# A three-block perceiver layer on one Trainium2 core: gathers on 64-column tiles, a first feed-forward product in two parts, weight loads and GpSimd's sums in another order

## The reference

```python
h = layernorm(x)
scores = einsum('bsd,d->bs', h, w_router)
top_scores, top_idx = top_k(scores, 32)            # 32 of the 64 rows of each batch
selected = h[top_idx]
y = gelu(selected @ W1 + b1) @ W2 + b2             # 512 -> 2048 -> 512
out = h; out[top_idx] += sigmoid(top_scores) * y
x = x + out
```

## Time and profile before

| | us |
|---|---|
| median of 3 runs | 1370.66 (1370.24 to 1371.76) |
| profiled execution, its own time | 1372.64 |
| span in the profile | 1370.8 |
| TensorE (PE) busy | 1335.4, 97% |
| VectorE (DVE) busy | 670.8, 49% |
| ScalarE (ACT) busy | 728.8, 53% |
| GpSimd (POOL) busy | 542.7, 40% |

### The profile page before, as it was taken

How to read it: one execution, slowest core, us unless ns; L and a number is a source line. 1 busy time by engine, 2 the same in 40 slices (tenths; PEclk the granted TensorE clock), 3 DMA queues, 4 the chain that set the end, 5 groups by cost and what they waited for, 6 DMA issues and landing times.

```text
span 1370.8 us, 33861 instructions
## 1 busy us (share of the span) xinstructions
PE 1335.4 (97%) x13368; PEld 1052.5 (77%) x13368; DVE 670.8 (49%) x1685; ACT 728.8 (53%) x1411; POOL 542.7 (40%) x284
## 2 busy tenths in 40 slices
PE   7999999999999999999999999999999998798998
PEld 5777777777777777777777777788888887587786
DVE  4244554554544544544544445457655686243323
ACT  6455655656656656656656566653433456233231
POOL 6542422422422422432332334725343443473442
PEclk9999999999999999999999999999999999899999
DMA  6011111010011010110110113010000002131331
GB/s 255 26 59 34 39 45 33 27 55 33 25 57 29 28 57 25 33 57 25 33 53 29 33 40 110 14 56 2 2 0 0 0 18 94 49 105 47 108 138 62
DMA packets 39335, 66.24 MB, mean 48 GB/s; under 512 B 4208, under 2 KB 8560, under 8 KB 39280
## 3 DMA queue, kind: packets, MB, share of 16 engines
q1 hardware_dynamic: 38848, 64.67, 14.6%
q10 hardware_dynamic: 432, 0.79, 0.2%
HBM read 61.25 MB, written 4.19 MB: 48 GB/s over the span
## 4 chain that ended last, share of the span: by engine, by line
PE 89%; POOL 2%; DVE 2%; ACT 1%; issue 1%; POOLq 0%; DVEq 0%
PE psum L205 39%; PE psum L962 9%; PE psum L253 8%; PE psum L1853 7%; PE psum L1884 6%; PE psum L223 5%; PE psum L241 5%; PE psum L977 3%; PE psum L262 3%; PE psum L987 1%; PE psum L995 1%; PE psum L1005 1%; POOL w_l L1407 1%; PE psum L1523 0%; PE psum L1864 0%
## 5 line engine op out<-in xcount | busy, mean ns | idle before, releaser
L303 ACT ACTIVATE PT<-psum 128x512 f32<-128x512 f32 x256 | 153.2, 598 | 226.5 <-PE psum L253 226.5
L290 ACT ACTIVATE prob<-prob,nmx 128x512 f32<-128x512 f32 x256 | 182.6, 714 | 94.4 <-DVE nmx L345 94.4
L359 DVE COPY V<-psum 128x512 f32<-128x512 f32 x128 | 88.6, 692 | 229.7 <-PE psum L205 229.7
L345 DVE CUSTOM_DVE_ANT_0 prob<-psum,mbias 128x512 f32<-128x512 f32 x256 | 165.5, 684 | 67.0 <-PE psum L223 67.0
L296 ACT ACTIVATE prob<-prob,rinv 128x512 f32<-128x512 f32 x256 | 182.6, 713 | 0.0
L492 POOL TENSOR_SCALAR ctx_a<-ctx_r 128x1536 fp32r<-128x1536 f32 x16 | 65.4, 4088 | 265.4 <-PE psum L205 265.2
L492 POOL TENSOR_SCALAR ctx_b<-ctx_r 128x1536 fp32r<-128x1536 f32 x16 | 65.4, 4088 | 251.8 <-PE psum L205 235.5
L253 PEld LDWEIGHTS psum<-ident,prob 128*128 128x128 f32 x1024 | 127.4, 141 | 34.8 <-issue 1.3
L253 PE MATMUL psum<-ident,prob 128*128 128x128 f32 x1024 | 153.3, 272 | 0.6 <-ACT PT L303 0.4
L205 PE MATMUL psum<-wv_h,ctx_b 128*128 128x512 f32 x384 | 144.4, 417 | 0.0
L205 PE MATMUL psum<-wv_h,ctx_a 128*128 128x512 f32 x384 | 142.2, 412 | 1.2 <-DVE K L359 1.2
(11 more groups left out here) (217 smaller groups left out, 2858.7 us busy)
## 6 DMA issues: line engine op xcount, KB each, us to landing
ctx_r<-in_ctx SPq DMA_DIRECT2D x32, 768.0 KB, 4.6
w_r<-in_L_ffn_W SPq DMA_DIRECT2D x64, 256.0 KB, 2.8
xres<-in_x SPq DMA_DIRECT2D x16, 256.0 KB, 2.6
out<-tok SPq DMA_DIRECT2D x13, 256.0 KB, 3.4
tok<-in_x SPq DMA_DIRECT2D x3, 1024.0 KB, 12.1
mask<-in_mask_BxS_bf SPq DMA_DIRECT2D x32, 64.0 KB, 4.1
tok<-in_x SPq DMA_DIRECT2D x4, 256.0 KB, 3.4
wq_r<-in_L_xattn_Wq SPq DMA_DIRECT2D x4, 256.0 KB, 4.5
```

The costliest lines, as they stand in the source:

```text
L290: act.activation(prob[:, r, :], prob[:, r, :], ACT.Exp, bias=nmx[:, r:r + 1], scale=-1.0, accum_out=rsum[:, r:r + 1]).then_inc(s_ex, 1)
L303: act.activation(PT[:, r, :, :].rearrange("p k n -> p (k n)"), T_bank, ACT.Copy).then_inc(s_Pt, 1)
L345: dve.tensor_tensor_reduce(prob[:, r, :], S_bank[r], mbias[:, b, :], 1.0, 3.0e38, ALU.add, ALU.min, nmx[:, r:r + 1]).then_inc(s_mx, 1)
L359: dve.tensor_copy(item_place(q, m), KV_bank[m % 2]).then_inc(s_KVe, 1)
```

## The change

- A gather uses two tiles of 64 columns of weights: 16 matmuls (32 records) in place of 32.
- `output_projection` of tile 13 is cut in two: its first half stays, the probabilities and the first gather follow, then the second half.
- The first feed-forward product, `hidden(0)`, is made in two parts of 256 columns into bank 4. The first part stands in `pe_end`, behind the gather (1, 0) and ahead of the last values, and waits for two `xs_l` parts (`s4_gl` 2) and the first `w_l`; the second stands where `hidden(0)` stood. Gelu of step 0 reads bank 4.
- Three of the `w_r` buffers lie at other places; loads 1 to 3 wait for the last keys (`s3_K`) and the values of tile 13 (`s3_PV`) in place of the last values' projection (`s3_V`). Ahead of all further loads SP waits until four gathers are done.
- GpSimd's sums stand at steps 2, 3, 13, 14 and 15, and wait for `s5_gl` of one step less.

```diff
--- before.py
+++ after.py
@@ -543,6 +543,7 @@
         qw_h = m("aq_h", [P, DT, D], F32R)
         qw_r = Map(nc, m.at)("aq_r", [P, DT, D], F32)
         qw_l = m("aq_l", [P, DT, D], F32R)
+        kw_h_at = m.at
         kw_h = m("ak_h", [P, DT, D], F32R)
         kw_r = Map(nc, ctx_end)("ak_r", [P, DT, D], F32)
         rope = m("rope", [P, 2, HD], F32)
@@ -970,9 +971,9 @@
                 ins = pe.transpose(place[:, k * P:(k + 1) * P], xn3[:, k * P:(k + 1) * P], ident[:])
             ins.then_inc(s3_XT, 1)
 
-        def output_projection(pe, buf, place=bank[2]):
-
-            for n in range(DT):
+        def output_projection(pe, buf, place=bank[2], parts=range(DT)):
+
+            for n in parts:
                 for i, (o, w) in enumerate(((o_h, ow_h), (o_h, ow_l), (o_l, ow_h))):
                     ins = pe.matmul(place, o[:, buf, n, :, :].rearrange("p b q -> p (b q)"), w[:, n, :],
                                     start=(n == 0 and i == 0), stop=(n == DT - 1 and i == PRODUCTS - 1))
@@ -1345,8 +1346,10 @@
         last_raw = m("w_r3", [P, 2, D], F32)
         assert m.at <= ctx_at + 24 * KB
         m = Map(nc, masks_end)
-        w_r = [m(f"w_r{e}", [P, 2, D], F32) for e in range(DEEP - 1)] + [last_raw]
-        assert m.at <= end2, (m.at, end2)
+        w_r = [m("w_r0", [P, 2, D], F32)]
+        m = Map(nc, kw_h_at)
+        w_r += [m("w_r1", [P, 2, D], F32), m("w_r2", [P, 2, D], F32), last_raw]
+        assert m.at <= kw_h_at + 4 * DT * D
 
         s4_xn = sem("p4_xn")
         s4_s, s4_dg, s4_R, s4_eq = sem("p4_s"), sem("p4_dg"), sem("p4_R"), sem("p4_eq")
@@ -1519,11 +1522,11 @@
             for k in range(DT):
                 for e in range(2):
                     mine = slice(e * BPG * KEEP, (e + 1) * BPG * KEEP)
-                    for r in range(4):
-                        ins = pe.matmul(bank4(c, 1 + h)[head_rows(r), k * P + mine.start:k * P + mine.stop],
-                                        xn4[:, SLOT_OF[c], 2 * h + e, k * P + r * HD:k * P + (r + 1) * HD],
+                    for r in range(2):
+                        ins = pe.matmul(bank4(c, 1 + h)[r * P // 2:(r + 1) * P // 2, k * P + mine.start:k * P + mine.stop],
+                                        xn4[:, SLOT_OF[c], 2 * h + e, k * P + r * P // 2:k * P + (r + 1) * P // 2],
                                         oh[:, c % 2, 2 * h + e, mine], start=True, stop=True,
-                                        tile_position=(0, r * HD))
+                                        tile_position=(0, r * P // 2))
             ins.then_inc(s4_G, 1)
 
         def pe_transpose(pe, c):
@@ -1537,6 +1540,17 @@
 
         LAST = G - 1
         PAR = LAST % 2
+
+        first_hidden = bank[4]
+
+        def hidden_part(pe, place, e, cols):
+
+            there = slice(cols.start % (4 * P), cols.start % (4 * P) + cols.stop - cols.start)
+            for k in range(DT):
+                for i, (w, y) in enumerate(((w_h, xs_h), (w_l, xs_h), (w_h, xs_l))):
+                    ins = pe.matmul(place[:, there], w[:, e, 0, k * P:(k + 1) * P], y[:, k, cols],
+                                    start=(k == 0 and i == 0), stop=(k == DT - 1 and i == PRODUCTS - 1))
+            return ins
 
         def pe_end(pe):
 
@@ -1555,12 +1569,13 @@
             pe.wait_ge(s3_ms, LAST)
             scores(pe).then_inc(s3_S, 1)
             pe.wait_ge(s3_x, LAST - 2)
-            output_projection(pe, PAR).then_inc(s3_Wo, 1)
+            output_projection(pe, PAR, parts=(0, 1))
             pe.wait_ge(s3_pn, LAST)
             pe.wait_ge(s3_v, G)
             for h in range(2):
                 probabilities(pe, 1 - PAR, h).then_inc(s3_PT, 1)
             pe_gather(pe, 0, 0)
+            output_projection(pe, PAR, parts=(2, 3)).then_inc(s3_Wo, 1)
             pe.wait_ge(s3_pa, 2 * LAST)
             values(pe, 1 - PAR).then_inc(s3_PV, 1)
             pe.wait_ge(s3_ms, G)
@@ -1575,9 +1590,11 @@
                 probabilities(pe, PAR, h).then_inc(s3_PT, 1)
             pe.wait_ge(s3_x, LAST - 1)
             pe_gather(pe, 1, 0)
+            pe.wait_ge(s4_gl, 2)
+            pe.wait_ge(s5_wl, 1)
+            hidden_part(pe, first_hidden, 0, slice(0, 2 * P))
             pe.wait_ge(s3_pa, 2 * G)
             values(pe, PAR).then_inc(s3_PV, 1)
-            pe.wait_ge(s4_gl, 1)
             pe_gather(pe, 1, 1)
             pe.wait_ge(s4_oc, 1)
             pe_transpose(pe, 1)
@@ -1678,9 +1695,11 @@
                 sp.dma_start(b2_sb[:], b2.rearrange("(a n) -> a n", a=1).broadcast_to([P, D])).then_inc(s4_c, 16)
                 sp.wait_ge(s3_XT, G)
                 load(sp, 0, 0, 0)
-                sp.wait_ge(s3_V, G)
+                sp.wait_ge(s3_K, G)
+                sp.wait_ge(s3_PV, G - 2)
                 for f in range(1, DEEP):
                     load(sp, f, f, f)
+                sp.wait_ge(s4_G, 2 * NCH // SC)
                 def store(q):
                     if q == 0:
                         return
@@ -1707,7 +1726,7 @@
                     pool.tensor_tensor(t, t, xn4_rows[:, bass.ds(row, 1), :].rearrange("p a n -> p (a n)"),
                                        ALU.add).then_inc(s4_tk, 1)
 
-                sums = {2: (0, 1), 3: (2, 3), 14: (4, 5), 15: (6, 7)}
+                sums = {2: (0,), 3: (1, 2), FF - 3: (3,), FF - 2: (4, 5), FF - 1: (6, 7)}
 
                 def split(f, n, e, q):
                     if isinstance(n, int) and n == 0:
@@ -1721,7 +1740,7 @@
                         pool.wait_ge(s5_gl, n - 1)
                         add(n + CH, n)
                     if isinstance(n, int) and n in sums:
-                        pool.wait_ge(s5_gl, n + 1)
+                        pool.wait_ge(s5_gl, n)
                         for t in sums[n]:
                             add(t, CH * SLOT_OF[t // CH] + t % CH)
 
@@ -1812,7 +1831,8 @@
                         split_high(act, n + EARLY, (e + EARLY) % DEEP)
                     act.wait_ge(s5_H, n + 1)
                     at_least(act, s5_gl, n - 1)
-                    act.activation(hid[:, e % 2, :], h_bank[e % 2], ACT.Gelu_apprx_tanh,
+                    place = first_hidden if isinstance(n, int) and n == 0 else h_bank[e % 2]
+                    act.activation(hid[:, e % 2, :], place, ACT.Gelu_apprx_tanh,
                                    bias=b1_sb[:, bass.ds(f, 1)]).then_inc(s5_g, 1)
                     if isinstance(n, int) and n in between:
                         between[n]()
@@ -1847,12 +1867,7 @@
                 def hidden(n, e, q):
                     pe.wait_ge(s5_wl, n + 1)
                     at_least(pe, s5_g, n - 1)
-                    for k in range(DT):
-                        cols = slice(q * 4 * P, (q + 1) * 4 * P)
-                        for i, (w, y) in enumerate(((w_h, xs_h), (w_l, xs_h), (w_h, xs_l))):
-                            ins = pe.matmul(h_bank[e % 2], w[:, e, 0, k * P:(k + 1) * P], y[:, k, cols],
-                                            start=(k == 0 and i == 0), stop=(k == DT - 1 and i == PRODUCTS - 1))
-                    ins.then_inc(s5_H, 1)
+                    hidden_part(pe, h_bank[e % 2], e, slice(q * 4 * P, (q + 1) * 4 * P)).then_inc(s5_H, 1)
 
                 def scatter(q, tiles):
 
@@ -1867,9 +1882,10 @@
                     if isinstance(f, int) and f == 0:
                         if q == 0:
                             pe.wait_ge(s4_gl, 2 * NCH // SC)
+                            hidden_part(pe, first_hidden, 0, slice(2 * P, 4 * P)).then_inc(s5_H, 1)
                         else:
                             pe.wait_ge(s4_gl, 2 * NCH)
-                        hidden(n, 0, q)
+                            hidden(n, 0, q)
                     if not (isinstance(f, int) and f == FF - 1):
                         hidden(n + 1, (e + 1) % DEEP, q)
                     if isinstance(n, int) and n in between:
```

## The result

| | before | after |
|---|---|---|
| median, us | 1370.45 (1370.06 to 1371.76, 4 runs) | 1351.82 (1351.07 to 1352.27, 4 runs) |
| profiled execution, own time | 1372.64 | 1351.07 |
| its span | 1370.8 | 1349.3 |
| TensorE busy | 1335.4, 97% | 1330.2, 99% |

The ratio is 0.9862, interval 0.9845 to 0.9879: 18.6 us faster by the medians. The two profiled executions differ by more, 21.6 us; why is worked out at the end.

A forecast was written before the change was run, and what follows sets the result against it. TensorE, busy 97%, was taken as the bound, so only its gaps and slow products could give time: 26.0 + 0.6 us removed, 3.6 added, 23.0 saved, 1370.7 - 23.0 = 1347.7 us; range 1343 to 1355.

The forecast's parts named there:

- GpSimd's sums: Feed-forward steps: with sums moved, TensorE's 12.6 us of waits for w_l go, and 7.2 us of slow products behind them.
- Stretch B: TensorE's chain from the second product of step 0 to the product behind step 15; holds the waits for w_l.
- slow products: Three feed-forward products behind waits for w_l, 5.50, 4.61 and 5.21 us, each forecast to return to 2.72: 7.2 us.
- Gaps in the gathers: Gaps of 3.28 and 1.68 us inside gathers, blamed on loads; moving those saves 5.0 us plus 1.2 of slow clock.
- Rival A: Gaps in the gathers stay, perhaps from density of instructions alone; 5.0 + 1.2 us back, 1353.9 us; chance 0.12.
- stretch A: TensorE's chain from the projection of tile 13 to the second product of step 0; holds the gaps in the gathers.
- Projection in halves: Tile 13's output projection, halved around probabilities and first gather: new waits of 0.2, 1.2 (dg) and 1.1 (o_l), 2.5 us.
- First product by chunks: First feed-forward product in 256-column parts: 0 to 2.7 us extra, 0 taken; a new 0.8 us wait for hid_l.
- Gathers' own time: Eight gathers with half the records, twice the columns: 0.95 us each against a spacing of 1.03, 0.6 us gained.
- Rival B: GpSimd and DVE collide: sums beside ranking and copies leave w_l of step 4 late; 1351.6 us; chance 0.07.
- C: Loads 4 and 5, behind the wait for the gathers, come late and TensorE still waits for w_l; 1367.5 us; chance 0.04.
- D: New short waits at 1137.8 to 1141 us drop the clock to 1.2 GHz into the feed-forward; slower than before; chance 0.04.

## Why the prediction was right, and where its sizes were off

The time, 1351.8 us, lies in the range of 1343 to 1355, and the direction is the forecast one. The saving was 18.6 us where 23.0 were forecast. By its steps:

1. **GpSimd's sums: right in mechanism, too large in size.** The three waits of 12.6 us fell to 0.4. The term was 12.6 + 7.2 = 19.8 us. The whole times give 16.4 (alone) and 16.5 (taken out of the change). Stretch B gives 18.5 (alone), 18.2 (on top of the gathers) and 17.2 (taken out of the change). The mis-sized part is the 7.2 us of slow products, which took 2.72 us for each product afterwards. The product behind the wait that is left takes 3.03 us (1174.76), and the one of step 15 takes 3.05 with no wait in front of it (1236.19). With the change's old sums the product behind the wait of 2.06 us took 3.02 us and not 4.61, so there 1.6 us less could be won. Why the medians give some 2 us less than stretch B is known in part: the execution of the sums alone lost more in its gaps, and the profiled execution of before was slower than its median (point 6).
2. **Gaps in the gathers: gone, by another cause.** The step that failed is "I read the gaps as TensorE's own instructions arriving late behind those loads". Loads alone left 1.43 and 0.94 us with no transfer running; gathers alone removed both. Rival A named the density and was wrong in what followed from it: the gaps did not stay, since the change also halves the number of instructions in a gather. The order listings, which the prediction had, show that. The size is partly luck: 6.2 us were taken and the medians of the gathers alone give 6.4, but by stretch A it was 6.5 against one execution of before and 4.4 against the other. The slow clock behind the first gap, put at 1.2 us, came in one of these two only. That the records come late because TensorE's instructions do is still argued; no row shows their arrival. The rule on turns between queues (the Trainium skill, DMA: Bandwidth & Descriptors, Queues, rings and completion order) spoke against loads as the only cause, and the runs bear that out, though the gaps were longer beside loads.
3. **Projection in halves: right.** dg and o_l were forecast for 1138.5 and 1140.3 and start at 1138.54 and 1140.30. TensorE came to them later than forecast, so its waits are 0.83 and 0.82 us where 1.2 and 1.1 were taken. The whole step was put at 2.5 us; it costs 2.6 by the medians and 2.2 in stretch A.
4. **First product by chunks: the sign was open, it costs.** The first chunk takes 1.62 us and the second some 1.4, where 2.72 was taken for both; the wait for hid_l came nearly as worked out (0.66 us for 0.8). With the wait for w_l that it leads to, the step costs 1.9 us. The work moved ahead is no gain, since ScalarE's chain from the last xs_h sets the first Gelu, and the chunk delays that xs_h.
5. **Gathers' own time: wrong sign.** 0.95 us was taken against 1.03, and 1.08 came. Eight of them lose 0.4 us where 0.6 was to be gained. The rule that the load's time goes with its columns (the Trainium skill, TensorE: Matmul & The Clock Gate, Part 2), by which the prediction had seen no gain, was nearer.
6. **The profiled execution and the median.** Between the two profiled executions 21.6 us are saved, near the 23.0. By stretches, A was forecast 3.2 us shorter (6.2 + 0.3 - 2.5 - 0.8) and came 3.3 shorter, in part by luck (point 2); B was forecast 19.8 shorter (19.8 + 0.3 - 0.3) and came 18.1 shorter (points 1 and 5). The rest is that the sum was made on one profiled execution and taken off the median. That of before was 2.2 us above the median of 1370.45, and that of after 0.7 below its own: 21.6 - 2.2 - 0.7 = 18.7. Part of the excess is slow clock: the second profile of before, 1.8 us shorter in its span, has 0.52 + 0.47 us less in spread and projection and 0.45 us less in the second gap.

Rival B came true in a small part: the one-hots were held up by w_l, which cost 0.4 us of waiting and not 2.0. C and D did not come; no wait of TensorE comes from the loads behind the wait for the gathers. Short waits can be followed by the low clock, as D had it and the kernel with old gathers shows, but by 1146 us it was back at 1.00.

Sums and gathers nearly add up: 16.4 and 6.4 us alone, 23.7 together. The whole change gives 19.2 us in the same group. The 4.5 us between are the 2.6 of the halved projection and the 1.9 of the chunks; the gaps that these, or the moved loads, might remove or shorten are gone already.

## What to carry to other kernels

A gap without a semaphore inside a run of very short matmuls was here a question of how many instructions stand in that run: try halving them before moving transfers. Test each remedy alone, since several remedies for one gap give its length once, and each keeps its own cost. A helper engine's filler work belongs where the engine's next product is not yet due, and its wait must not name a result later than it needs: the two lines of that edit were worth over 16 us. Where a bound engine's clock can fall behind a wait, take the size of the fall from several executions, not from one profile. And compare traces stretch by stretch, so that a cost that comes and goes elsewhere in the program does not hide what a step is worth.

## What the runs showed of the hardware that was not expected

- The low clock behind a gap can differ between executions of one kernel. Behind the gap of 3.28 us spread and projection took 1.15 and 3.23 us in one, 0.63 and 2.76 in the other. Between kernels: a wait of 2.0 us was followed by a product of 4.61 and 4.62 us in the two traces of before, of 3.02, 3.07 and 3.02 in three others. Waits of 0.9 and 0.8 us were followed by 4.61 in one kernel, waits of 0.8 and 0.8 by 3.03 in another.
- Gathers with half the instructions and twice the columns of weights take 5% longer each (1.08 against 1.03 us), but end the gaps, which stood 255 records apart in all four traces that have them.
- A one-hot pair on VectorE (one input tensor, from SBUF) took 1.60 us beside GpSimd's subtraction and 0.60 alone. That subtraction, 2.31 us in the earlier trace rows, took 2.82 at step 4.
